# x1's product and the suffix sums moved to other units of a fused attention and expert kernel

## The reference

```python
xn = layernorm(x)
# branch 1: attention with 16 heads of width 8, weights W*, causal
p    = where(causal, -10000, q @ k.T * 8**-0.5);  e = (p - threshold) / tau
attn = 1 - tanh(e)**2;  attn = attn / (sum(attn) + 1e-6)
s    = (attn @ v) @ Wo.T
# branch 2: attention and a mixture of experts
h  = rmsnorm(xn, norm1_w)
x1 = xn + softmax(q2 @ k2.T * 8**-0.5) @ v2 @ wo
h2 = rmsnorm(x1, norm2_w)                       # x1 * 1/sqrt(mean(x1*x1) + 1e-6) * norm2_w
g  = silu(x1 + swiglu(h2, shared) + sum_e combine_e * swiglu(h2, expert_e))   # 8 experts, top 2
out = x + s * g
```

## Time and profile before

| | |
|---|---|
| Time, median of 3 runs | 1099.15 us (1097.03 to 1099.39) |
| The profiled execution: its own time | 1097.14 us |
| Its span | 1095.4 us |
| TensorE busy | 990.9 us (90%) |
| VectorE busy | 831.4 us (76%) |
| ScalarE busy | 646.8 us (59%) |
| GpSimd busy | 351.2 us (32%) |
| Granted TensorE clock | 0.98 of full speed over the span |

### The profile page before, as it was taken

The page is one execution under the profiler, slowest core; times in us unless marked ns, Lnnn a source line. Parts: engine busy times, 40 slices in busy tenths (PEclk is TensorE's granted clock), DMA queues, the critical chain, the costliest instruction groups (busy, mean ns, idle before and its releaser), DMA issues.

```text
span 1095.4 us, 18252 instructions
## 1 busy us (share of the span) xinstructions
PE 990.9 (90%) x6763; PEld 467.3 (43%) x6784; DVE 831.4 (76%) x1684; ACT 646.8 (59%) x882; POOL 351.2 (32%) x211
## 2 busy tenths in 40 slices
PE   4489999899998999889998999989999899988997
PEld 1123464245542455324652346523554245532464
DVE  6885977869776888759878598795977779773962
ACT  3569724786258842698336972379624785258731
POOL 4702443033520355105530154203352033610032
PEclk9589999999999999999999999999999999999999
DMA  7350561023700435105331055211471033600020
GB/s 231 71 109 22 111 169 34 21 55 80 190 20 12 99 93 132 30 2 130 112 83 30 2 130 143 51 31 30 101 181 24 21 79 83 163 20 2 1 79 10
DMA packets 60392, 81.83 MB, mean 75 GB/s; under 512 B 8560, under 2 KB 47728, under 8 KB 57296
## 3 DMA queue, kind: packets, MB, share of 16 engines
q1 hardware_dynamic: 56544, 75.61, 28.3%
q10 hardware_dynamic: 3760, 5.05, 1.4%
HBM read 52.98 MB, written 27.39 MB: 73 GB/s over the span
## 4 chain that ended last, share of the span: by engine, by line
PE 53%; DVE 25%; ACT 12%; issue 4%; DMA 2%; SPq 1%; ACTq 0%; POOL 0%; DVEq 0%; POOLq 0%
PE O L1156 11%; DVE nmax L758 10%; DVE PT L813 9%; PE O L1139 7%; ACT PT L613 7%; PE S L1172 6%; PE S L1174 5%; PE S L1173 5%; PE S L1112 4%; PE M L1075 3%; PE M L1054 2%; PE M L1080 1%; PE O L1075 1%; SPq L368 1%; DMA stackQ<-mTZ 1%
## 5 line engine op out<-in xcount | busy, mean ns | idle before, releaser
L613 ACT ACTIVATE PT<-S 128x1024 f32<-128x1024 f32 (+1 forms) x448 | 417.0, 967 | 113.7 <-PE S L1112 108.7
L813 DVE SCALAR_TENSOR_TENSOR PT<-PT 128x768 f32<-128x768 f32 (+1 forms) x192 | 213.4, 1163 | 101.0 <-ACT PT L613 101.0
L758 DVE TENSOR_REDUCE nmax<-M 128x1 f32<-128x512 f32 x329 | 218.2, 684 | 43.2 <-PE M L1075 28.3
L1139 PE MATMUL O<-PT,V 128*32 128x256 f32 (+3 forms) x2816 | 246.5, 430 | 0.0
L494 POOL TENSOR_TENSOR PT<-PT,CB 128x1024 f32<-128x1024 f32 x56 | 133.6, 2392 | 261.2 <-DVE PT L951 146.9
L646 ACT ACTIVATE PT<-S 128x1024 f32<-128x1024 f32 x72 | 73.9, 1027 | 241.4 <-PE S L1174 241.4
L479 POOL TENSOR_TENSOR split<-split,parts 128x512 f32<-128x512 f32 x30 | 90.9, 3029 | 372.0 <-ACT parts L573 372.0
L1112 PE MATMUL S<-stackQ,stackK 64*128 64x512 bf16 (+3 forms) x1024 | 166.3, 347 | 9.5 <-DMA stackQ<-mTZ 5.3
L758 DVE TENSOR_REDUCE nmax<-O 128x1 f32<-128x512 f32 x183 | 125.1, 684 | 36.5 <-PE O L1075 17.6
L1172 PE MATMUL S<-h2hi,wgu_hi 128*128 128x512 f32 x288 | 148.7, 516 | 4.3 <-DVE PT L951 4.2
L1156 PE MATMUL O<-PT,wdn 128*128 128x512 f32 x288 | 142.9, 595 | 0.9
(11 more groups left out here) (198 smaller groups left out, 1044.5 us busy)
## 6 DMA issues: line engine op xcount, KB each, us to landing
CB<-scrC SPq DMA_DIRECT2D x64, 256.0 KB, 5.6
stackQ<-scrQ SPq DMA_DIRECT2D x30, 384.0 KB, 5.5
stackK<-scrK SPq DMA_DIRECT2D x30, 384.0 KB, 6.3
scrQ<-parts SPq DMA_DIRECT2D x32, 192.0 KB, 3.3
scrK<-parts SPq DMA_DIRECT2D x30, 192.0 KB, 5.9
scrQ<-parts SPq DMA_DIRECT2D x32, 128.0 KB, 3.4
scrK<-parts SPq DMA_DIRECT2D x30, 128.0 KB, 5.2
KX<-scrK SPq DMA_DIRECT2D x14, 192.0 KB, 3.4
```

The lines of the kernel that those rows point to most:

```text
L613: a.activation(PT[:, n % SLOTS, 2 * q * w:2 * q * w + 2 * w].rearrange("p (r n) -> p r n", r=2), S[k][:, :].rearrange("p (r n) -> p r n", ...
L758: v.tensor_reduce(nmax[:, h % 2, h // 2, t:t + 1], M[k][:, :], AX.X, ALU.max, negate=True).then_inc(m_read[k], 1)
L813: v.scalar_tensor_tensor(p, p, 1.0, p, ALU.subtract, ALU.mult).then_inc(weighed, 1)
L1139: last = t_.matmul(O[k][32 * q:32 * q + VW, i0:i1], V[:, j, 4 * g + q, :], PT[:, n % SLOTS, w * q + at:w * q + at + i1 - i0], start=(j == ...
```

## The change

It has three parts.

1. x1's product moves from the row's end to unit 26, sub-step 3, ahead of the transposes of h2t. O[0] is opened there by a product of zeros (64 rows, bf16, 512 columns: KX's unused rows), so that the four products and all experts add to it. `down_done` counts nine steps a row.
2. The scaling of x1 by the inverse root moves from VectorE (unit 24) to ScalarE (unit 25, behind the OS copy, ahead of Q1's reads), which waits for a new semaphore `rooted`.
3. The suffix's seven products move from expert 0 to units 11 to 14, one block each behind the first scores; VectorE's multiplication by the constants moves to the end of stage 1, and `corr` gets memory of its own. In units 11 to 15 the V product is issued in one piece at sub-step 3.

```diff
-PLACES[EXPERT] += ["suffix"]
+PLACES[11] += ["suffix"]
-DOWNS = NE + 1
+DOWNS = NE
-        corr = h2T[:, :].rearrange("p (t d) -> p t d", t=NT)
+        corr = sb("corr", [128, NT, D])
 # ScalarE, weights()
-                done = {0: 0, 1: 1, 2: DEPTH}
-                if q == 0 and n in done and it * DOWNS + done[n] > 0:
+                done = {0: 1, 1: 2, 2: DEPTH}
+                if q == 0 and n in done:
 # ScalarE, row(), behind acc_out
+                    if n == 25:
+                        act.wait_ge(rooted, it + 1)
+                        for t in range(NT):
+                            last = a.activation(h2t[:, t, :], x1[:, t, :], ACT.Copy, scale=rinv[:, 2, t:t + 1])
+                        last.then_inc(h2_ready, 1)
 # VectorE, row()
                 for n in range(N1):
                     for name in u.places[n]:
-                        take(u, it, name)
+                        if name != "suffix":
+                            take(u, it, name)
...
                     norm_apply(bt)
+                take(u, it, "suffix")
                 for n in range(N1, UNITS):
...
                         inverse_root(rinv[:, 2, :], root[:, 2, :], newton[:, 0, :])
-                        for t in range(NT):
-                            last = v.tensor_scalar(h2t[:, t, :], x1[:, t, :], rinv[:, 2, t:t + 1], None, ALU.mult)
-                        last.then_inc(h2_ready, 1)
+                        dve.sem_inc(rooted, 1)
...
                     if e == 0:
-                        take(u, it, "suffix")
                         combine(it)
 # TensorE
+            def x_turned(u, it):
+                pe.wait_ge(*read(u, "proj2"))
+                pe.wait_ge(o_read[0], it * O_USES[0] + 3)
+                pe.wait_ge(kset, 4)
+                t_.matmul(O[0][:, :], identb[HALF:128, :], KX[HALF:128, 0, 0, :], start=True, stop=False)
+                for t in range(NT):
+                    t_.matmul(O[0][:, t * 128:t * 128 + 128], x1[:, t, :], ident[:, :], start=False, stop=False)
 # second_product(): no wait on o_read[0] at e == 0
-                                     start=(e == 0 and f == 0), stop=(e == NE - 1 and f == NFH - 1))
+                                     start=False, stop=(e == NE - 1 and f == NFH - 1))
+            def later_sums(u, t):
+                k, _n = u("suffix")
+                last = t_.matmul(M[k][:, t * 128:t * 128 + 128], below[:, :], V1c[:, t, :], start=True, stop=(t == NT - 1))
+                if t < NT - 1:
+                    rest = V1c[:, t + 1, :] if t == NT - 2 else VS[:, t, :]
+                    t_.matmul(M[k][:, t * 128:t * 128 + 128], ones[:, :], rest, start=False, stop=True)
+                else:
+                    last.then_inc(m_full[k], 1)
 # TensorE, row()
+                        elif 11 <= n < N1:
+                            if i == 3:
+                                with_v(it, v_at[n])
                         elif v_at.get(n, N1) < N1 and v_at[n] % NT > 0:
...
+                        if n == 26 and i == 3:
+                            x_turned(u, it)
                         for name in now:
                             work(u, it, name)
+                        if i == 0 and 11 <= n < 11 + NT:
+                            later_sums(u, n - 11)
...
-                for t in range(NT):
-                    last = t_.matmul(O[0][:, t * 128:t * 128 + 128], x1[:, t, :], ident[:, :], start=False, stop=False)
-                last.then_inc(down_done, 1)
                 for _step in second_product(it, NE - 1):
                     pass
```

More of the change, by code:

```diff
@@ L266, in program @@
         xn_ready, h_ready, h2_ready, h2r_ready = (sem(n) for n in ("xn_ready", "h_ready", "h2_ready", "h2r_ready"))
-        squared = sem("squared")
+        squared, rooted = sem("squared"), sem("rooted")
         exps_ready, gap_ready, top_ready, comb_ready = (sem(n) for n in ("exps_ready", "gap_ready", "top_ready", "comb_ready"))
@@ L1145, in with_v @@
                     last.then_inc(pv_done, 1)
+            def x_turned(u, it):
[5 more added lines that the diff above has]
+                    t_.matmul(O[0][:, t * 128:t * 128 + 128], x1[:, t, :], ident[:, :], start=False, stop=False)
             def second_product(it, e):
                 if e == 0:
-                    pe.wait_ge(o_read[0], it * O_USES[0] + 3)
                     k, c = score_use(it, 2 * EXPERT + 1)
@@ L1249, in work @@
                     pe.wait_ge(v_summed, it * 2 + 2)
-                    k = begin(u, name)
-                    for t in range(NT):
[L1252 to L1256, removed]
+                    begin(u, name)
                 elif name == "combT":
```

## The result

The changed kernel is slower: 1107.39 us (median of 4, 1105.81 to 1108.33) against 1099.27 us (median of 4 beside it, 1097.03 to 1101.33). The ratio is 1.0083, 95% interval 1.0070 to 1.0096. I had forecast 1094.4 us. The profiled execution took 1106.66 us with a span of 1104.9 us; that of before 1097.14 and 1095.4. So the spans differ by 9.5 us.

What follows compares the result with a forecast made beforehand. TensorE was taken to bound the experts, ScalarE stage 1's second half, VectorE then ScalarE stage 2. Seven rows (-3.4 us) and the last (-1.3) gave -4.7: 1092.4 us profiled, 1094.4 us median; range 1089 to 1099.5.

Steps and rivals of the forecast that it cites:

- ScalarE's chain is 1.6 us later: Stage 2: four scaling copies put off Q1's reads, and h2hi, the logits and TensorE's first expert with them; other end 2.2 us.
- +1.6 - 1.48 = +0.12 us at expert 1: TensorE in the experts: ScalarE's 1.6 us delay less the suffix's 1.48 us removed from expert 0 leaves +0.12 us.
- Part 1, -1.09 us: Row's end: removing x1's product lets VectorE's maxima start 1.09 us earlier each row; ends -1.09 and -0.5 us.
- the overhang before h2T: At x1's product's new place: transposes start at about 516.25 us, no cost since ScalarE reads later; uncovered, at most 0.5 us.
- Part 2, copies: ScalarE between OS copy and Q1's reads: four scaling instructions, 0.27 us start to start, 0.43 us long, after some 0.4 us idle.
- Part 3, stage 1, +0.33 us: Units 12 to 14: suffix records make TensorE fall behind ScalarE, +0.33 us a row; ends 0 and +0.9 us.
- Part 3, expert 2, +0.27 us: VectorE's product of expert 1, then expert 2's second half, come 0.27 us later a row; ends -0.2 and +0.9 us.
- The last row, -1.3 us: Last row, with no Q1 to read: -0.7 us kept of VectorE's savings, -0.89 us of x1, +0.33 us of stage 1.
- The sum at full clock: A middle row: -1.09 + 0.33 + 0.27 = -0.49 us, times seven = -3.4 us.
- units 12 to 15 become TensorE's: Rival, chance 0.10: ScalarE runs dry in stage 1, +1.8 us there, row +0.9 us, 1106 us; decides above 1.15 us lost.

Runs made afterwards that it cites:

- part 3 alone: Kernel before with only the suffix in pieces in units 11 to 14 and V there in one piece: 1098.59 us against 1098.89, ratio 0.9994.
- part 1 alone: Kernel before with only x1's product moved to unit 26: 1091.61 us against 1098.89, ratio 0.9928; run again, 1090.53 us against 1098.60.
- part 2 alone: Kernel before with only the scaling of x1 moved to ScalarE: 1136.65 us against 1098.89, ratio 1.0327.

## Why the prediction was wrong

**The step that failed** is in part 2: "ScalarE's chain is 1.6 us later", and the time handed on from there with nothing added, "+1.6 - 1.48 = +0.12 us at expert 1". The chain was 1.76 us later. What it set off wasn't in the sum: TensorE, waiting behind it, lost its clock. With the idle time filled by products of zeros the changed kernel is 5.8 us faster, and 7.7 us of the 9.5 us between the profiled executions lie in the three rows with half clock. The clock is one half of the miss. The profiled execution came out 14.3 us above the 1092.4 us that I had summed for it: 7.7 us are the clock, and the other 6.5 us are terms of the sum at full clock, part 3's in stage 1 above all, with the 0.7 us of rows 2 and 6 in it that the traces don't explain. I had written that x1's product fills TensorE's wait, and took the idle time that part 2 makes longer only as cover for that product. No rival spoke of the clock, though the granted clock stood in every window that I read.

By the steps:
- **Part 1, -1.09 us**: right in kind; 0.88 us measured, alone and in the change. 0.2 us went to the second product, 1.93 in place of 1.73 us now that x1's product no longer stands ahead of it. The product of zeros and the overhang before h2T cost nothing, as said.
- **Part 2, copies**: 0.386 us each, 0.30 us from start to start, 1.28 us in all behind a wait of 0.47 us; said were 0.43 us each, 0.27 from start to start, 1.24 in all and 0.4. h2hi 5.33 us behind OS; said was 5.2. The rule of the Trainium skill that gives multiplications to VectorE ("ScalarE: Activation LUTs", rules for kernel authors) came out right here, for a reason beyond the price of the instruction: ScalarE was the chain there. The estimate of 1.27 us from the prices of the same page of the Trainium skill ("What ACT_TABLE_LOAD costs") is within 0.02 us of the 1.28 us measured.
- **Part 3, stage 1, +0.33 us**: 0.87 us measured. The block's entry is 0.22 us and not 0.05, which makes 0.34 us in two units; the other 0.2 us are the overlap that ScalarE loses at its two stops.
- **Part 3, expert 2, +0.27 us**: 22.48 us from x1 to VectorE's product of expert 1 before, 22.91 after at full clock, +0.43.
- **The last row, -1.3 us**: -0.97 us. **The first row**, which I counted as a middle one, came out at -0.35 us: its stage 1 was only 0.1 us longer.
- **The sum at full clock**: a middle row +0.44 us (row 5) where I had -0.49. So I would have been wrong without the clock too, by 0.93 us a row: the changed kernel with products of zeros is 0.2% slower than before, not 0.4% faster. Three mis-sized terms, all one way (0.21, 0.54, 0.16 us).
- **The rivals**: "units 12 to 15 become TensorE's" gave 1106 us, near the measured time by luck. Its stretch lost 0.87 us a row, less than the 1.15 us that I had given as the point from which it decides, and part 3 alone is no slower than before.

What stays open: why three of seven rows lost the clock in the profiled execution and four with the same schedule did not. The granted clock over the span, 0.974 to 0.976 in all four executions of the changed kernel, points to falls in each of them, but only one was traced. The opening moves that mean too: TensorE runs at half clock there for a time that differs between executions (mean clock of the first 90 us 0.79 in the profiles of the kernel before and the changed one, 0.73 in that with part 2 undone, whose mean over the span is 0.977 without any fall in mid-run). So executions of one kernel spread by some us (of those of the kernel before beside part 1 alone, a mean clock of 0.983 goes with 1096.4 to 1098.0 us and one of 0.977 with 1101.4 to 1102.8 us), and small differences are better read from rows. Nor do the runs tell a wait from the short products around it: products of zeros filled the waits and left the work around them as it was.

## What to carry to other kernels

Before work goes to another engine, look at which engine the chain runs through at that place, not at which is less busy on average: ScalarE had 59% over the span and none to spare between x1 and h2hi. Where the move lengthens waits of TensorE that stand close together, put a price on its clock: 0.34 us more idle time in 5.40 us went with falls in three rows of seven. Fill the waits with work that must be done anyway: with x1's product in that place three rows lost the clock, in part 2 alone, without it, all seven did. Work that is to be hidden has to fit a wait with its entry: seven products in one wait gained 0.2 us a row, the same seven in two waits 0.86 us.

## What the runs showed of the hardware

GpSimd and VectorE trade time in ways that busy sums hide. The subtraction that splits Q1's projection (L479) took 8.19 us in the kernel before and 1.71 us in the changed one. In the kernel before VectorE went on at its usual pace, and the subtraction ended at 523.93 us, 0.3 us after VectorE's first gap. In the changed kernel VectorE had no gap beside it either, but its own instructions were longer: four products in a row took 5.07 us in place of 4.09, h2lo 1.52 in place of 0.68. The rows of before, then those of after:

```profile
515.60 4.09 DVE L813 SCALAR_TENSOR_TENSOR PT<-PT 128x768 f32<-128x768 f32 x4
515.74 8.19 POOL L479 TENSOR_TENSOR split<-split,parts 128x512 f32<-128x512 f32 x1 [11.24 <-ACT parts L573]
...
519.61 0.68 DVE L937 TENSOR_TENSOR h2lo<-h2T,h2hi 128x512 fp32r<-128x512 f32 x1
...
523.63 0.35 DVE L818 RECIPROCAL lq<-lq 128x32 f32<-128x32 f32 x1 [0.41 <-ACT lq L638]
```

```profile
519.44 5.07 DVE L818 SCALAR_TENSOR_TENSOR PT<-PT 128x768 f32<-128x768 f32 x4
...
521.98 1.71 POOL L479 TENSOR_TENSOR split<-split,parts 128x512 f32<-128x512 f32 x1 [12.97 <-ACT parts L573]
...
524.42 1.52 DVE L942 TENSOR_TENSOR h2lo<-h2T,h2hi 128x512 fp32r<-128x512 f32 x1
```

GpSimd's busy time fell from 351.2 to 311.0 us, while VectorE's products of this kind rose from 213.4 to 227.0 us. The difference comes with part 2: the thirty instructions of L479 take 90.9 us in the kernel before and with part 1 or part 3 alone, 46.1 us with part 2 alone. h2hi to the first expert's product is 4.30 us at full clock (4.32 before), so the longer h2lo costs nothing there. Why one order holds GpSimd up and the other VectorE, no run shows.
